# Projection and attention of a transformer block put into one instruction block, with attention's first loads ahead of projection's last stores

## What is computed

```python
xn = layernorm(x)                      # 8 x 1024 x 256
q, kv = xn @ Wq, xn @ Wkv              # keys and values are the same projection
q, kv = rotary(q), rotary(kv)
p = softmax(scale * q @ kv.T)          # per sequence and head, 1024 x 1024
x = x + (p @ kv) @ Wout + bout
x = x + experts(layernorm(x))          # gate, the 1024 best tokens of each of 8 experts, two-layer FFN
```

## Time and profile before

| | us |
|---|---|
| median of 3 runs | 2415.57 |
| lowest and highest | 2413.13, 2423.36 |
| the profiled execution, its own time | 2414.75 |
| the profiled execution, its span in the trace | 2412.9 |
| projection's last instruction (VectorE) | at 238 |
| first maxima of attention | at 287 |
| end of attention | about 1630 |

### The profile page before, as it was taken

How to read it: one execution, slowest core, us unless ns; L and a number is a source line. 1 busy time by engine, 2 the same in 40 slices (tenths; PEclk the granted TensorE clock), 3 DMA queues, 4 the chain that set the end, 5 groups by cost and what they waited for, 6 DMA issues and landing times. The chain is left out here.

```text
span 2412.9 us, 52712 instructions
## 1 busy us (share of the span) xinstructions
PE 2064.1 (86%) x16812; PEld 1057.0 (44%) x16812; DVE 1996.3 (83%) x3156; ACT 1495.9 (62%) x2850; POOL 669.3 (28%) x848
## 2 busy tenths in 40 slices
PE   6776199999999999999999999993897139999898
PEld 3343033333333333333333333331454128888798
DVE  7887299999999999999999999953676787888874
ACT  4444068888888888888888888880333013443333
POOL 7887000000000000000000000001675035566664
PEclk9999589999999999999999999996898559999999
DMA  3676512222222222222222222206673023333332
GB/s 102 221 226 198 150 28 58 56 60 60 59 59 60 60 60 60 60 60 60 60 55 56 57 55 56 60 30 136 220 249 128 0 84 68 93 83 81 85 67 29
DMA packets 128508, 207.85 MB, mean 86 GB/s; under 512 B 16935, under 2 KB 89130, under 8 KB 128426
## 3 DMA queue, kind: packets, MB, share of 16 engines
q1 hardware_dynamic: 116142, 189.84, 27.7%
q0 software_dynamic: 12288, 17.05, 4.3%
HBM read 121.06 MB, written 84.67 MB: 85 GB/s over the span
## 5 line engine op out<-in xcount | busy, mean ns | idle before, releaser
L640 DVE TENSOR_REDUCE a_mx<-a_sm 128x2 f32<-128x1024 f32 x1024 | 1235.2, 1223 | 113.2 <-PE a_sm L588 97.2
L709 ACT ACTIVATE a_prob<-a_st 128x512 f32<-128x512 f32 x2048 | 1113.4, 597 | 164.8 <-PE a_st L551 133.2
L588 PE MATMUL a_sm<-a_k,a_q 48*128 48x512 f32 x2048 | 753.7, 457 | 57.7 <-DMA a_k<-qkv_parts 50.0
L551 PE MATMUL a_st<-a_q,a_k 50*128 50x512 f32 x2048 | 755.1, 450 | 0.0
L575 PE MATMUL a_pv<-a_prob,a_v 128*32 128x256 f32 x8192 | 655.8, 392 | 22.9 <-ACT a_oraw L716 22.3
L551 PEld LDWEIGHTS a_st<-a_q,a_k 50*128 50x128 f32 x2048 | 310.4, 185 | 404.1 <-ACT a_prob L709 391.0
L575 PEld LDWEIGHTS a_pv<-a_prob,a_v 128*32 128x32 f32 x8192 | 161.8, 108 | 401.7 <-issue 192.8
L588 PEld LDWEIGHTS a_sm<-a_k,a_q 48*128 48x128 f32 x2048 | 303.6, 188 | 70.9 <-DMA a_k<-qkv_parts 50.4
L682 POOL TENSOR_TENSOR a_v<-a_v_raw,a_zero 128x256 f32<-128x256 f32 x64 | 39.8, 622 | 926.2 <-DMA a_v_raw<-values 911.7
L1705 ACT ACTIVATE e_hT<-e_ps_h,e_b1b 128x512 f32<-128x512 f32 x128 | 88.3, 690 | 274.6 <-PE e_ps_h L1739 268.7
L1739 PE MATMUL e_ps_o<-e_w_high,e_hT_high 128*128 128x256 f32 x512 | 151.6, 296 | 29.0 <-DVE e_biased L1610 29.0
(11 more groups left out here) (149 smaller groups left out, 2403.6 us busy)
## 6 DMA issues: line engine op xcount, KB each, us to landing
qkv_parts<-p_parts SPq DMA_DIRECT2D x64, 512.0 KB
a_q<-qkv_parts SPq DMA_DIRECT2D x128, 128.0 KB, 2.7
a_k<-qkv_parts SPq DMA_DIRECT2D x128, 128.0 KB, 2.9
attended<-a_oraw SPq DMA_DIRECT2D x64, 256.0 KB, 2.8
e_w<-in_fc_dram SPq DMA_DIRECT2D x16, 1024.0 KB
token_table<-f_tab SPq DMA_DIRECT2D x8, 1056.0 KB, 8.7
p_x<-in_x_dram SPq DMA_DIRECT2D x16, 512.0 KB, 8.1
values<-p_values SPq DMA_DIRECT2D x8, 1024.0 KB, 19.7
```

Of the source, the lines that this page charges most:

```text
L551: nc.tensor.matmul(st[:, slot % RING], kb[rows, q.buf, jt * P:(jt + 1) * P], qb[rows, q.buf, ic * CHUNK:(ic + 1) * CHUNK], start=True, sto ...
L588: mm = nc.tensor.matmul(sm[:, slot, h], qb[rows, q.buf, qt * P:(qt + 1) * P], kb[rows, q.buf, kc * CHUNK:(kc + 1) * CHUNK], start=True, st ...
L640: nc.vector.tensor_reduce(mx[:, qt, kc, :], sm[:, slot], AX.X, ALU.max, negate=True).then_inc(max_done, 1)
L709: nc.scalar.activation(prob[:, jt % 2, h, ic * CHUNK:(ic + 1) * CHUNK], st[:, slot % RING], ACT.Exp, scale=DH ** -0.5).then_inc(drained, 1)
```

## The change

Projection and attention share one block. `project` and `attend` no longer open blocks; each returns its five engine programs, and a new function `project_and_attend` runs them one after the other on every engine.

- **No barrier.** The SBUF buffers of both stages exist side by side. Projection's six PSUM banks are given back for attention; instead of the barrier, TensorE waits before its first maxima until projection's tiles have been read out of PSUM (`banks_free`).
- **SP's order.** After `store(2, 1)` SP waits for the landing of `store(0, 0)`, then issues attention's identity, the loads of q0, q1 and q2 and the rows of ones (`load_first`), and only then `store(3, 0)` and `store(3, 1)`. The wait for the landing of all stores (`stored`) stands in the body of q0, before `max_rows` of q1.
- **q0's turned maxima** are issued by ScalarE (`max_rows(act, ...)`), into ScalarE's DMA queue.
- **Set-up.** GpSimd's memsets of attention come first in its program (`set_buffers`). `a_ones` is one row block of 1024 in place of three; the transfer repeats it.

The diff, cut to its core (the rest is the same text at another indentation):

```diff
-def project(nc, x, w_qkv, rot_cos, rot_sin, ident_d, parts_dram, v_dram):
+def project(nc, ctx, x, w_qkv, rot_cos, rot_sin, ident_d, parts_dram, v_dram):
...
+    with ExitStack() as own:
+        banks = Alloc(nc, own)
+        ps_xT = banks.ps("p_ps_xT", [P, 2, 4, P])
+        ps_q = banks.ps("p_ps_q", [P, 2, 4 * P])
+        ps_rT = banks.ps("p_ps_rT", [P, 2, 4, P])
...
         store(PASSES - 2, 1)
+
+        sp.wait_ge(parts_out[0], 16 * 4 * CUTS)
+        sp.wait_ge(v_out[0], 16)
+        load_first(sp)
         for s in range(SEQS):
             store(PASSES - 1, s)
+
+    def stored(sp):
+
         for s in range(SEQS):
             sp.wait_ge(parts_out[s], 16 * 4 * CUTS * PASSES)
             sp.wait_ge(v_out[s], 16 * PASSES)
+
+    def banks_free(pe):
+
+        pe.wait_ge(xnT_done, STEP * PASSES)
+        pe.wait_ge(qkv_done, STEP * PASSES)
+        pe.wait_ge(high_done, STEP * PASSES)
+        pe.wait_ge(low_done, STEP * PASSES)
...
-        ones = a.sb("a_ones", [CUTS, 3, N])
+    ones = a.sb("a_ones", [CUTS, N])
...
+    def max_rows(eng, q, turned):
+
+        eng.wait_ge(drained, turned + 1)
+        rows = CUTS * TILES
+        for h in range(2):
+            top = HEAD_ROWS * h + DATA_ROWS
+            eng.dma_start(qb[top:top + CUTS, q.buf, :].bitcast(F32).rearrange("r (t c) -> r t c", c=P),
+                          mrow[h * rows:(h + 1) * rows, :]).then_inc(m_in, 16)
+
+    def load_first(sp):
+        sp.dma_start(ident[:], ident_d).then_inc(ident_in, 16)
+        for p in range(3):
+            load(sp, Pair(0, p, p))
+        sp.wait_ge(set_up, 4)
+        for h in range(2):
+            top = HEAD_ROWS * h + DATA_ROWS
+            sp.dma_start(kb[top:top + CUTS].bitcast(F32), ones[:].unsqueeze(1).to_broadcast([CUTS, 3, N])
+                         ).then_inc(ones_in, 16)
...
+        def body(q):
+            if q.first():
+                stored(sp)
+            elif q.plus(2).exists():
+                load(sp, q.plus(2))
+            if not q.first():
+                store(q.plus(-1))
+            if q.plus(1).exists():
+                max_rows(sp, q.plus(1), turn_of(q)[1])
...
+        q0, q1 = Pair(0, 0, 0), Pair(0, 1, 1)
+        banks_free(pe)
...
+        copy_max_rows(Pair(0, 0, 0), 0, 0)
+        max_rows(act, Pair(0, 0, 0), 0)
+        pairs(act, body)
...
+        @block.gpsimd
+        def _(pool):
+            set_buffers(pool)
+            first.gpsimd(pool)
+            second.gpsimd(pool)
...
-        project(nc, t["x"], t["w_qkv"], t["rot_cos"], t["rot_sin"], t["ident"], parts, values)
-        attend(nc, parts, values.rearrange("b r p n -> (b r) p n"), o, t["ident"])
+        project_and_attend(nc, t, parts, values, o)
```

More of the change, by code:

```diff
@@ L391 @@
+    return Stage(sync, tensor, vector, scalar, gpsimd), stored, banks_free
 CHUNK = 512
@@ new lines, in pairs, with fill_of, turn_of, head_rows @@
+    def pairs(eng, body):
+        body(Pair(0, 0, 0))
+        with eng.Fori(0, (NP - 4) // 3) as k:
+            for c in range(1, 4):
+                body(Pair(k, c))
+        for p in range(NP - 3, NP):
+            body(Pair(0, p, p))
+    def fill_of(q, u):
+        turns = 1 if u >= TURN_FILL and q.plus(1).exists() else 0
+        return 1 + u + turns, q.n * FILLS + (1 + u + turns)
+    def turn_of(q):
+        return 1 + TURN_FILL, q.n * FILLS + (1 + TURN_FILL)
+    def head_rows(h, rows):
+        return slice(HEAD_ROWS * h, HEAD_ROWS * h + rows)
@@ new lines, in load @@
+    def load(sp, q):
+        if not (q.p is not None and q.p < 3):
+            sp.wait_ge(filled, 1 + (q.n - 2) * FILLS)
+        for h in range(2):
+            for kind, (buf, runs) in enumerate(((qb, Q_RUNS), (kb, K_RUNS))):
+                for row, part, parts in runs:
+                    row += HEAD_ROWS * h
+                    sp.dma_start(buf[row:row + parts * DH, q.buf, :].bitcast(F32),
+                                 parts_dram[bass.ds(q.n * 2 + h, 1), kind, part:part + parts]
+                                 .rearrange("o s d n -> (o s d) n")).then_inc(qk_in[q.buf], 16)
+        if not (q.p is not None and q.p < 3):
+            sp.wait_ge(v_placed, q.n - 2)
+        sp.dma_start(v_raw[:, q.buf].rearrange("p i h e -> p (i h e)"),
+                     v_dram[bass.ds(q.n, 1)].rearrange("o p n -> (o p) n")).then_inc(v_in[q.buf], 16)
@@ new lines, in vector, with reduce, body @@
+    def vector(dve):
+        def reduce(q, v, s, slot):
+            qt, kc = v // 2, v % 2
+            if v == 0 and not q.first():
+                dve.wait_ge(nm_done, q.n)
+            dve.wait_ge(sm_done, s + 1)
+            nc.vector.tensor_reduce(mx[:, qt, kc, :], sm[:, slot], AX.X, ALU.max,
+                                    negate=True).then_inc(max_done, 1)
+            if v == NG - 1:
+                if not q.first():
+                    dve.wait_ge(n2_done, q.n)
+                dve.wait_ge(max_done, (q.n + 1) * NG)
+                nc.vector.tensor_tensor(nm[:], mx[:, :, 0], mx[:, :, 1], ALU.min).then_inc(nm_done, 1)
+        def body(q):
+            for g in range(NG):
+                ahead = q.plus(1) if g < NG // 2 else q.plus(2)
+                if ahead.exists():
+                    reduce(ahead, (g + NG // 2) % NG, q.n * NG + AHEAD + g, g % 2)
+        for v in range(NG):
+            reduce(Pair(0, 0, 0), v, v, v % 2)
+        for v in range(NG // 2):
+            reduce(Pair(0, 1, 1), v, NG + v, v % 2)
+        pairs(dve, body)
@@ new lines, in set_buffers, with gpsimd, split, place @@
+    def set_buffers(pool):
+        nc.gpsimd.memset(zero[:], 0.0).then_inc(set_up, 1)
+        nc.gpsimd.memset(vb[:], 1.0).then_inc(set_up, 1)
+        nc.gpsimd.memset(nsplit[:].bitcast(F32), 0.0).then_inc(set_up, 1)
+        nc.gpsimd.memset(ones[:], 1.0).then_inc(set_up, 1)
+    def gpsimd(pool):
+        def split(q):
+            part = [nsplit[:, 0:2 * CUTS * TILES].rearrange("p (h s t) -> p s t h", h=2, s=CUTS)[:, s]
+                    for s in range(CUTS)]
+            pool.wait_ge(nm_done, q.n + 1)
+            if not q.first():
+                pool.wait_ge(filled, 1 + (q.n - 1) * FILLS)
+            nc.gpsimd.tensor_tensor(part[0], nm[:], zero[:], ALU.add).then_inc(n1_done, 1)
+            pool.wait_ge(n1_done, q.n + 1)
+            nc.gpsimd.tensor_tensor(part[1], nm[:], part[0], ALU.subtract).then_inc(n2_done, 1)
+        def place(q):
+            pool.wait_ge(v_in[q.buf], (q.turn + 1) * 16)
+            if not (q.p is not None and q.p < 3):
+                pool.wait_ge(pv_done, (q.n - 2) * TILES)
+            nc.gpsimd.tensor_tensor(vb[:, q.buf, :, :, 0:DH], v_raw[:, q.buf],
+                                    zero[:].unsqueeze(3).to_broadcast([P, TILES, 2, DH]), ALU.add
+                                    ).then_inc(v_placed, 1)
+        def body(q):
+            split(q)
+            if not q.first() and q.plus(2).exists():
+                place(q.plus(2))
+        pool.wait_ge(set_up, 4)
+        for p in range(3):
+            place(Pair(0, p, p))
+        pairs(pool, body)
```

927 lines of the change are left out of this document (417 added, 510 removed).

## The result

The changed kernel takes 2381.6 us (median of 4 runs, 2368.0 to 2390.0) against 2415.7 for the kernel before: ratio 0.985, interval 0.981 to 0.990. In two later comparisons, one on chip 15 and one on chip 2, it stood at 0.986 (0.983 to 0.989) and 0.983 (0.980 to 0.987). The forecast was 2376, with a range of 2363 to 2386; its ratio would be 0.984. The gain is 34 us in 2416.

The account below looks back on a forecast made before the run. The prediction took the seam between projection and attention to be bound by transfers. From 2414.75 us it took 48.4, added 6.0 for a stall and 3.0 for the clock: 2375.4, or 2376 as a median, range 2363 to 2386.

Parts of the forecast that it names:

- The hole and its cause: Seam between projection and attention: 40 us with TensorE, VectorE and ScalarE idle, bound by transfers of 5.24 MB.
- First maxima at 238.9: Attention's start: TensorE's first maxima wait only for projection's last PSUM read, at 238.9 instead of 287.3, gaining 48.4 us.
- `load_first` issued by 217.7: SP's queue behind store(2, 1): issuing attention's first loads starts at 203.3, takes 14.4 us and ends at 217.7.
- Stores pushed back by 12.9 us, to 292.0: Projection's last stores: 2.88 MB of loads ahead of them delay the landing of all stores from 279.1 to 292.0.
- q1 at 296.0 after a stall of 6 us: q1's first score: its rows wait for the stores' landing, so it starts at 296.0 instead of 290.0.
- ScalarE's rows at 0: Before q0's first score: turned maxima issued by ScalarE cost 0, having 6.0 us of cover less 1.3 for issuing.
- rival B: Before q0's scores: ScalarE's transfers queue behind SP's, scores start 14.3 us late; 2381, or 2394 behind all stores; chance 0.12.
- The clock at 3.0: Start of q1: TensorE's half clock after the 6 us idle costs 3.0 us, the middle of 1.3 and 4.8.
- A: Before q1: no stall, as loads fill gaps and stores land by about 286; 2362 to 2367 us; chance 0.20.
- C: At the seam: q0's loads land only with the stores behind them, maxima start at 292; 2420 us; chance 0.02.
- D: Attention's loop: reductions slow by 0.050 us each because tiles have other places in SBUF; 2427 us; chance 0.02.
- The sum: Whole run: 2414.75 less 48.4, plus 6.0, plus 3.0, gives 2375.4; the median is 0.8 higher, so 2376.

Follow-up runs that it names:

- the repetitions: The changed kernel run again unaltered, in two later comparisons: medians 2388.0 and 2379.9 us, against 2421.2 and 2422.4 for the kernel before.
- the held store: Against the changed kernel, SP waits until q0's turned maxima have landed before it issues store(3, 1): 2384.8 us, ratio 0.983 to the kernel before.

## Why the prediction was right, and where it was not

- **The hole and its cause.** Right. The run with the loads behind the stores and the one with the loads ahead and a wait show that barrier and queue order are one cause: the stores' landing, and the loads behind it.
- **First maxima at 238.9.** 240.7 in the first profile, where projection itself ended 1.8 us later; 238.0 and 239.6 in the repetitions.
- **`load_first` issued by 217.7.** Wrong: SP was through at 231.3. The step that failed is "Its issue took 14.4", taken from a moment when the queue was empty. Right behind a full sequence's store the first transfer alone blocks SP for 12.56 us (10.99 to 12.85 in all the runs that issue it there, 11.69 behind the last store). It cost at most about 1 us here: `store(3, 0)` was issued 13.5 us later (231.37 for 217.84), yet all stores landed only 0.3 to 1.3 us after the forecast's 292.0.
- **Stores pushed back by 12.9 us, to 292.0.** Right: 292.8, 292.3 and 293.3 in three profiles, 13.2 to 14.2 later than 279.1.
- **q1 at 296.0 after a stall of 6 us.** The time was right (295.75 in the first profile, some 3 and 7 us later in the repetitions), the reason was not. The stall in front of q1 was 0.66 us. What I had put there was spent earlier: 1.8 us at projection's end, and 3.5 us in front of q0. That these and the 0.66 add up to the forecast's 6.0 is luck.
- **ScalarE's rows at 0.** Wrong, and half of rival B in its place: they landed 9.7, 12.8 and 13.0 us after the issue began in the three profiles, and q0 idled for 3.5, 6.6 and 6.8 us. The step that failed is the 2.7 us of a load's landing, a row without a full queue. It holds for that case: the held store shows 3.3 us with the queue nearly dry. Of the two rules of the Trainium skill ("DMA: Bandwidth & Descriptors", Queues, rings and completion order) the turn-taking between queues, by which the forecast's term was 0, does not agree with the 9.7 to 13.0 us for two transfers of 8 KB. The other one, that a signal lands after the engine's earlier writes from any queue, goes in the right direction. That it is the mechanism is argued here, not shown.
- **The clock at 3.0.** The place was wrong, and the size. I charged it to an idle before q1 that did not occur. At q0's body I took the 11 us at half clock of the earlier trace rows as given; it was 11, about 20 and 24 us in the three profiles of the changed kernel, 11 and 20 in the two of the kernel before, and 37 us in the run with half the stores. At 0.43 us lost per us that is 4.7 to 16 us in a single run. Between the two kernels it nearly cancels, as far as five profiles can tell, and the forecast had no term for its spread.
- **Rivals.** A's sign came true, its reason did not: q1 idled only 0.66 us, and not at all for the stores in the repetitions, but because it came late itself; the stores landed at 292 to 293 and not by 286. B's nearer value was 2381, and the median is 2381.6; that is luck too, since B had q0 start 14.3 us late and the rows cost 3.5 to 6.8. C and D are out: the maxima start at once, and a reduction still takes 1.223 us.
- **The sum.** 39.4 us were forecast, 34.1 measured by the medians. The last attention store gained 39.7 between the means of the profiles. That this meets the 39.4 so closely is partly luck, since the idles and the clock were not where they were forecast. What separates it from the medians' 33 to 43 us is no more than the spread of the tail, 781.8 to 806.1 us, which the forecast took as fixed.

## What to carry to other kernels

Removing a barrier and putting the next stage's loads ahead of the last stores were one change here, and each half alone was worth nothing: ask of every wait at a seam what stands in front of it in the transfer queue. Take the issue time of a transfer from a row where the queue was as full as it will be, and expect queued data to slow a small transfer on the critical path even from another engine's queue (8 to 14 us here, against 3.3). Before believing a gain of 10 us after a seam, look at the granted clock on both sides of it in more than one profile.

## What was not expected

- A last store that begins 17 to 18 us later need not land much later: held back, it was issued in 12.0 instead of 27.6 us and landed only about 2.5 us later (295.2). 12.4 of the 27.6 us are its first transfer, right behind the store of values of the sequence before, as with the 12.56 us of the first load in `load_first`:

```profile
244.00 12.43 SPq L180 DMA_DIRECT2D qkv_parts<-p_parts  x1
```

- TensorE at 100% busy time in the record for 39 us (241 to 280) kept the half clock, while in other profiles the clock was full again after 9 to 11 us of q0's body, which is as busy in the record. What decides it stays open.
- The medians of the kernel before ranged from 2412.8 to 2426.6 us over the comparisons, and on one chip (15) they were 2421.2 and 2426.6. A time says little without the kernel before beside it.
